# The passage from weight composition to the first batch in a four-layer residual kernel: masks asked for as their places come free, and a reordered first group

## The reference

```python
x = x + (x @ W0.T + b0 + coeff[b] * (x @ (2 * mask[b] - 1)))    # layer 0, mask[b]: 1024x1024 int32
x = x + x @ w_eff.T                                             # layer 1: w_eff from weight, scale, codebook, LoRA
x = x + (x @ W2 + b2 + 2.0 * (x @ A2[tok]) @ B2[tok])           # layer 2 (W as 'bti,io')
x = x + 1.0 * ((x @ B3[tok].T) @ A3[tok].T)                     # layer 3
```

## Time and profile before

| | us |
|---|---|
| median of 3 executions | 548.01 |
| lowest, highest | 547.4, 548.13 |
| the profiled execution | 548.42 |
| its span (first to last instruction) | 546.5 |
| TensorE busy in it | 531.0 |
| VectorE, ScalarE, GpSimd busy | 459.9, 351.4, 170.8 |

### The profile page before, as it was taken

The page is one execution under the profiler, slowest core; times in us unless marked ns, Lnnn a source line. Parts: engine busy times, 40 slices in busy tenths (PEclk is TensorE's granted clock), DMA queues, the critical chain, the costliest instruction groups (busy, mean ns, idle before and its releaser), DMA issues.

```text
span 546.5 us, 9011 instructions
## 1 busy us (share of the span) xinstructions
PE 531.0 (97%) x2864; PEld 458.3 (84%) x2864; DVE 459.9 (84%) x742; ACT 351.4 (64%) x681; POOL 170.8 (31%) x170
## 2 busy tenths in 40 slices
PE   4999999999998999999999999999999999999997
PEld 4988788888887888888888888888888888888886
DVE  5998898898963979987999889897898987989853
ACT  3777775786754874685767657667676665766730
POOL 2669878997723340003004003000300400400120
PEclk9999999999999999999999999999999999999999
DMA  8767031843487793458347455746834645564222
GB/s 231 244 90 153 21 119 60 242 140 116 98 192 259 243 355 60 151 194 165 134 143 187 94 177 170 119 151 194 164 135 156 169 110 174 170 103 156 76 50 77
DMA packets 147281, 82.57 MB, mean 151 GB/s; under 512 B 105060, under 2 KB 124516, under 8 KB 147124
## 3 DMA queue, kind: packets, MB, share of 16 engines
q1 hardware_dynamic: 145444, 78.34, 51.5%
q0 software_dynamic: 1520, 3.86, 2.7%
q10 hardware_dynamic: 288, 0.01, 0.0%
HBM read 65.93 MB, written 16.26 MB: 150 GB/s over the span
## 4 chain that ended last, share of the span: by engine, by line
PE 78%; DVE 13%; ACT 4%; DMA 3%; issue 1%; POOL 0%; SPq 0%; DVEq 0%; ACTq 0%; POOLq 0%
PE bank L1698 19%; PE bank L1705 10%; PE bank L1572 5%; PE bank L1574 5%; PE bank L1573 5%; PE bank L1742 5%; PE bank L1741 5%; PE bank L1740 5%; PE bank L1791 3%; PE bank L1789 3%; PE bank L1790 3%; DVE merged_ring L1226 3%; PE bank L1753 2%; PE bank L1482 2%; DVE m_lo L1232 1%; DVE w_lo L1133 1%
## 5 line engine op out<-in xcount | busy, mean ns | idle before, releaser
L1698 PE MATMUL bank<-x_t_pair,m_hi 128*128 128x512 f32 x512 | 128.6, 393 | 2.5 <-ACT m_hi L835 2.5
L615 POOL TENSOR_TENSOR x_t_pair<-x_sum,x_t_pair 128x256 fp32r<-128x256 f32 x32 | 29.8, 958 | 283.7 <-ACT x_t_pair L910 283.7
L1698 PEld LDWEIGHTS bank<-x_t_pair,m_hi 128*128 128x128 f32 x512 | 92.5, 189 | 20.2 <-ACT m_hi L835 3.3
L835 ACT CAST m_hi<-merged_ring 128x512 fp32r<-128x512 f32 x128 | 73.0, 619 | 55.0 <-PE bank L1705 28.0
L1232 DVE TENSOR_TENSOR m_lo<-merged_ring,m_hi 128x512 fp32r<-128x512 f32 x128 | 84.5, 708 | 9.1 <-ACT m_hi L835 9.0
L825 ACT ACTIVATE merged_ring<-mask_ring,batch_now 128x1024 f32<-128x1024 int32 x62 | 75.5, 1242 | 19.7 <-DMA mask_ring<-in_mask_Bx4096x_ik 18.7
L1226 DVE TENSOR_TENSOR merged_ring<-merged_ring,w_t 128x1024 f32<-128x1024 f32 x64 | 75.9, 1212 | 14.2 <-ACT merged_ring L825 10.7
L1705 PEld LDWEIGHTS bank<-x_t_pair,m_lo 128*128 128x128 f32 x512 | 69.8, 190 | 5.0
L1705 PE MATMUL bank<-x_t_pair,m_lo 128*128 128x256 f32 x512 | 71.4, 282 | 0.0
L1742 PE MATMUL bank<-P_hi,x_t_pair 128*128 128x496 f32 x160 | 61.4, 384 | 0.0
L1741 PE MATMUL bank<-P_lo,x_t_pair 128*128 128x496 f32 x160 | 61.4, 384 | 0.0
(11 more groups left out here) (223 smaller groups left out, 1115.0 us busy)
## 6 DMA issues: line engine op xcount, KB each, us to landing
mask_ring<-in_mask_Bx4096x_ik SPq DMA_DIRECT2D x62, 512.0 KB, 4.0
w_nat<-in_L_cond_W SPq DMA_DIRECT2D x14, 512.0 KB, 5.1
x_t_squares<-in_x SPq DMA_DIRECT2D x56, 128.0 KB, 2.9
w_raw<-in_L_cond_weight SPq DMA_DIRECT2D x16, 256.0 KB
out<-out_staged SPq DMA_DIRECT2D x16, 248.0 KB, 4.8
w0t_dram<-w_out SPq DMA_DIRECT2D x14, 256.0 KB, 3.0
w_t<-w0t_dram SPq DMA_DIRECT2D x6, 512.0 KB, 6.4
g_batch<-g_dram POOLq DMA_DIRECT2D x21, 128.0 KB, 4.2
```

Of the source, the lines that this page charges most:

```text
L835: nc.scalar.copy(Mh[:, n % MR], ring_f[:, k % MR, h * HALF:(h + 1) * HALF]).then_inc(s["h_set"], 1)
L1698: mm(bank[L0_BANK[HT * h + j]][:, :], Mh[:, n % MR, j * P:(j + 1) * P], xThl[:, :, :, k + i, :], start=(k + i == 0), stop=False, skip_grou ...
```

## The change

It moves instructions and changes five numbers of waits; nothing is computed otherwise.

- SP: mask pair 3 is asked for right after pair 1 (its own wait stays), pair 5 right after the store of W0's last half, before pair 2, and pair 4 last. The `w0t` loads ask for the exact number of used blocks of their column half, and go out in the order 0, 4, 1, 2, 3.
- ACT: the copy of W0's last half goes ahead of the last `w1_hi`; `signs(0, 2)` ahead of the x copies, whose first two wait for block 3 instead of 4 and whose last two for block 4 instead of 5; `signs(0, 3)` ahead of `m_hi(0, 0)`; `p_hi(7, [0])` behind `m_hi(0, 1)`.
- DVE: `w0_eye` ahead of the last `w1_lo`; `merged(0, 0)` between the two `x_lo_first`; `m_lo(0, 1)` ahead of `p_lo(7, [0])`.
- POOL: its two x parts wait for `p_used` too.
- First group: ACT does `p_hi(0, [0])` ahead of `mid_up(4)` and `a3_set(0)` right after P's other parts; DVE does `p_lo(0, [0])` between the last two terms of half 4.

```diff
@@ load_w0t
-                sp.wait_ge(s["p_used"], KT * (G - 1) + (4 * last + 16) // 5)
+                end = 4 * last + (10 if j < HT else 12)
+                sp.wait_ge(s["p_used"], KT * (G - 1) + (end + 4) // 5)
@@ sync
             load_mask(0, 1)
+            sp.wait_ge(s["w0_tr"], 2 * (G - 1))
+            load_mask(0, 3)
             sp.wait_ge(s["eff_set"], 2 * G)
             load_mask(0, 0)
             store_w0t(blk, 1)
+            sp.wait_ge(s["p_used"], KT * (G - 1))
+            sp.wait_ge(mask_in[1], 16)
+            load_mask(0, MR + 1)
             for h in range(2):
                 sp.wait_ge(w0_out_stored[h], 16 * (G - 1))
             load_mask(0, 2)
...
-            for j in range(HT):
+            for j in (0, HT, 1, 2, 3):
                 load_w0t(j)
@@ gpsimd
                 pool.wait_ge(s["xt_hi"], i + 1)
+                pool.wait_ge(s["p_used"], KT * (G - 1) + i + 2)
@@ scalar, half(n)
                 scaled(n - 1)
+                if n == 4:
+                    p_hi(0, range(1))
                 mid_up(n)
                 if n == 4:
-                    p_hi(0)
+                    p_hi(0, range(1, 3))
+                    a3_set(0)
...
                 w1_hi(n - 1)
-                if n == 4:
-                    a3_set(0)
@@ vector, terms_up(n)
                 term(5, term_c[:, :]).then_inc(s["terms"], 1)
+                if n == 4:
+                    p_lo(0, range(1))
@@ vector, half(n)
                 if n == 4:
-                    p_lo(0)
+                    p_lo(0, range(1, 3))
```

More of the change, by code:

```diff
@@ L424, in _ @@
             load_mask(0, 2)
-            sp.wait_ge(s["w0_tr"], 2 * (G - 1))
-            load_mask(0, 3)
             sp.wait_ge(s["w1_ready"], 2 * G)
@@ L430, in _ @@
             load_mask(0, MR)
-            sp.wait_ge(s["p_used"], KT * (G - 1))
-            sp.wait_ge(mask_in[1], 16)
-            load_mask(0, MR + 1)
-            for j in range(HT):
+            for j in (0, HT, 1, 2, 3):
                 load_w0t(j)
@@ L473, in first_batch @@
                 for k in range(MR):
-                    load_w0t(k + MR)
+                    if k:
+                        load_w0t(k + MR)
                     if k > 1:
@@ L812, in _ @@
             scaled(2 * G - 1)
+            w0_evac(G - 2, 1)
             w1_hi(2 * G - 1)
-            w0_evac(G - 2, 1)
             p_hi(G - 2)
@@ L885, in _ @@
                 signs(0, k)
+            signs(0, 2)
+            act.wait_ge(s["p_used"], KT * (G - 1) + 3)
+            x_hi(0, range(2))
             act.wait_ge(s["p_used"], KT * (G - 1) + 4)
-            x_hi(0, range(2))
-            act.wait_ge(s["p_used"], KT * (G - 1) + 5)
             x_hi(0, range(2, 4))
-            signs(0, 2)
+            signs(0, 3)
             m_hi(0, 0, True)
+            m_hi(0, 1, True)
             p_hi(G - 1, range(1))
-            signs(0, 3)
-            m_hi(0, 1, True)
             signs(0, MR)
@@ L1206, in _ @@
             effective(2 * G - 1)
+            w0_eye(G - 2)
             w1_lo(2 * G - 1)
-            w0_eye(G - 2)
             dve.wait_ge(s["late_in"], 32)
@@ L1258, in x_lo_first @@
                 nc.vector.tensor_tensor(xTl[:, i % 2, ks, :], xs0[:, i % 2, ks, :], xTh[:, i % 2, ks, :].bitcast(F32), ALU.subtract).then_inc(s["xt_first"], 1)
+            dve.wait_ge(s["p_used"], KT * (G - 1) + 4)
+            x_lo_first(0)
+            merged(0, 0, True)
             dve.wait_ge(s["p_used"], KT * (G - 1) + 5)
-            x_lo_first(0)
             x_lo_first(1)
-            merged(0, 0, True)
             m_lo(0, 0)
             merged(0, 1, True)
+            m_lo(0, 1)
             p_lo(G - 1, range(1))
-            m_lo(0, 1)
             def out_add(b, i, plain=False, first=False):
```

## The result

| | before | after |
|---|---|---|
| median of 20 executions | 548.24 us | 549.79 us |
| lowest, highest | 547.4, 549.59 | 548.3, 551.37 |
| the profiled execution, its span | 548.42, 546.5 | 550.46, 548.6 |
| mean granted clock in it | 1.000 | 0.994 |

The ratio is 1.0026, with a 95% interval of 1.0018 to 1.0034: 1.4 us slower. The prediction said 545.3 us, at most 546.9, and gave "slower" a chance of 0.05. It was wrong in sign.

A forecast was written before the change was run, and what follows sets the result against it. TensorE, busy 531.0 of 546.5 us, was taken as the bound, its passage before layer 0 bound by late-started transfers. Passage 2.1 plus first group 0.6 made 2.7 us: 548.01 to 545.3 us, range 544.2 to 546.9.

The forecast's parts named there:

- The sum of bytes: Passage: bytes queued ahead of `w0t` 0, at 311 GB/s, land it 1.7 us sooner, at 173.0; 172.5 was taken.
- The first group: First group: A3's earlier copy gains 0.6 us; the 0.6 us from `P_lo` are given back at `delta`.
- From the fourth step on nothing is lost or won: Layer 0: matmuls run without a gap from the fourth step, so its gain, 2.1 us, reaches the end.
- `w0t` 0 lands at 172.5: Passage: the first `w0t` part lands at 172.5 instead of 174.7, bounds 170.3 and 174.7.
- the hole at 163: Passage: DMA engines idle from 163 to 164; earlier mask requests fill this microsecond, worth 0.3 MB.
- L: Passage: landing of `w0t` 1, put at 175.4, between 173.8 with a dry queue and 175.9 with a full one.
- R2: Rival, passage: the queue is the bound, `w0t` 4 first costs 1.7 us, total 546.2 to 547.1 us; chance 0.19.
- The store lands at about 164, mask 2 at 168: Passage: the W0 store lands at about 164, against 163.0 before, and mask 2 3.9 us later, about 168.
- R4: Rival, passage: slower; late mask 2 holds up ScalarE and the first step, deciding from 171.5 on; 549.9 us; chance 0.05.
- mask 2 + 5.2 = 173.2 < 174.86: Passage: ScalarE's work after mask 2 takes 5.2 us, ending 1.7 us before the first step's turn.
- From a landing the first `merged` takes 1.2 us (row 1.23): Passage, VectorE: `merged` takes 1.2 us after a `w0t` landing, then half of `m_hi` 0.6, before the step starts.
- Step 3 at `merged(0, 1)` + 5.8: Layer 0: step 3 starts at L + 5.8 = 181.2, from `merged` 1.2 and ScalarE's work 4.6, 0.8 us late.

The follow-up runs named there:

- SP's order alone: SP's new order of masks and `w0t` loads, on the kernel before with the first group's part of the change: ratio 0.9989.
- with VectorE's x parts: The changed kernel with GpSimd's two x parts made by VectorE, ahead of `merged(0, 0)`: ratio 1.0004 to the kernel before.
- with fillers: The changed kernel with eight matmuls that nobody reads, between the composition and layer 0: ratio 1.0028 to the kernel before.
- GpSimd's parts held back: The kernel before with the first group's change, GpSimd's x parts waiting for the first `w0t` part: ratio 1.0030, against 0.9994 without the wait.
- `signs(0, 2)` undone: The changed kernel with ScalarE's `signs(0, 2)` back behind the x copies: ratio 1.0009 to the kernel before.
- engines alone: The changed kernel with SP's order as in the kernel before: ratio 1.0008 to the kernel before.
- VectorE's order: The changed kernel with both of VectorE's x terms ahead of the first `merged`: ratio 1.0042 to the kernel before.
- passage alone: The changed kernel without the first group's part of the change: ratio 1.0044 to the kernel before.

## Why the prediction was wrong

Two steps failed. The sum of bytes had `w0t` 0 land at 172.5, and it landed at 173.84; with this alone the kernel is level with the one before (1.0004 without GpSimd's two parts). The 1.2 us of the first `merged` were 2.14, since GpSimd stood in its way; this made the kernel slower.

**The first group: right in the trace.** 0.6 put, 0.73 there, with the 0.6 of `P_lo` given back at `delta` as worked out (0.42 us of wait for `effective(3)`). In the timed runs it was 0.3 us, not told apart from nothing.

**From the fourth step on nothing is lost or won: right** for the changed kernel (360.2 us against 360.3). In the traces of the experiments the rest of the span was 360.3 to 362.0 us. Where it was long, TensorE had waits for `m_hi` that the kernel before has shorter or not at all: 0.76 us at 197.86 and 0.90 at 245.66 with both x terms and the x copies ahead, against 0.35 at 244.44 before. So a fourth step that comes sooner is not all gain, and whether the order or chance makes these waits is open.

**"`w0t` 0 lands at 172.5": wrong, mis-sized by 1.4 us.** The request went out at 166.58, as forecast (166.4). It took 7.3 us. The step that failed is the sum of bytes: I took 311 GB/s for the ten microseconds behind the hole, and they moved 230. (The sum gave 173.0; the 0.5 us that I took off had no row behind them.) Filling the hole at 163 won nothing, since SP then stood behind the store and left another at 165. The transfers asked for first became longer, the store 7.6 us and not 4.1, mask 2 4.8 and not 3.9, `w0t` 0 7.3 and not 6.5; masks 4 and 5 became shorter (7.5 and 5.4, from 8.1 and 8.9). SP's order alone brought neither `w0t` part forward. Why the DMA engines moved fewer bytes at the same busy share stays open.

**L, the landing of `w0t` 1: 175.4 put, 176.46 measured.** It was asked for at 169.17, 0.73 us sooner than before, and took 7.3 us instead of 6.1. So `w0t` 4 ahead of it cost 1.2 us, and L lies in R2's range. The Trainium skill (DMA: Bandwidth & Descriptors, "Anatomy of one DMA"), quoted for 3.2 us, gives that price for transfers that GpSimd issues. SP issues these, and this one took 7.3 us.

**"The store lands at about 164, mask 2 at 168": the first 0.6 us late, the second 1.5.** R4's mechanism was there (store behind two more masks, ScalarE behind mask 2), though at 169.5 it stood below the 171.5 that R4 asked for. The sum "mask 2 + 5.2 = 173.2 < 174.86" priced ScalarE's own chain and stopped. ScalarE did end `signs` 3 at 173.98, ahead of the end of `merged`. What it lacked is who else reads the x copies: GpSimd's two parts, which began 1.8 us later than before (172.40, 170.56).

**"From a landing the first `merged` takes 1.2 us (row 1.23)": the step that turned the sign.** A duration read from a trace in which `merged` came first was used in a schedule in which GpSimd did. In the kernel before GpSimd had been done with its parts for 1.2 us; it began a copy 0.44 us behind `merged`, which kept its 1.23 us, and the next two `m_lo` took 1.49 and not 1.29. So the sign of the turns was in that trace, unread:

```profile
170.56 3.00 POOL L620 TENSOR_TENSOR x_t_pair<-x_squares_first,x_t_pair 128x512 fp32r<-128x512 f32 x2 [16.08 <-ACT x_t_pair L845]
175.16 1.81 POOL L625 COPY w_t<-w_last 128x512 f32<-128x512 f32 x2 [1.61 <-PE bank L1574]
176.63 1.49 DVE L1232 TENSOR_TENSOR m_lo<-merged_ring,m_hi 128x512 fp32r<-128x512 f32 x2 [0.68 <-ACT m_hi L835]
```

In the changed kernel the first `merged` took 2.14. The x term moved behind it was priced at nothing and took 1.09, and delayed `m_lo` and the second `merged`, which came at 178.56; L was then no bound at all (the part had landed at 176.46). That the x term and two `m_lo` stand between the two `merged` was not in the formula for step 2 and 3: with VectorE's x parts the second `merged` came at 177.51, 3.8 us behind the first, again with its part long there. By my formula the first step would have come at 173.86 + 1.2 + 0.6 = 175.7. `merged` added 0.9, and the x term, whose end at 177.02 the first step also wanted, 0.5 more: 177.12 (in the traces with fillers and with VectorE's x parts, too, the first step starts 0.10 us behind the x term). The fourth step's 2.16 us of delay, and the 0.73 us of the first group that it swallowed, are 2.9 us; 1.2 of these are the low clock of this one execution, the other 1.7 the late start and what the same turns did to `merged(0, 1)`.

**Step 3 at `merged(0, 1)` + 5.8: right as a formula.** With `merged(0, 1)` at 178.34 in the kernel with fillers, step 3 came at 184.05, 5.7 later. Only its start was wrong.

**R2**, the queue as the bound, was the likeliest of the rivals. It held for SP's part: L lay between its 176.3 and 177.2. None of the rivals had VectorE's and GpSimd's turns. R4, the only one that said "slower", named the late mask 2 that set them up, but not them. The text said that the moved waits "put idle time in another place" and never asked which engine would meet which in that place.

## What to carry to other kernels

Moving an instruction in time changes its neighbours, and a duration from a trace holds only with the neighbours that it had. Before you move an input of GpSimd's work, lay its new stretch beside VectorE's critical instructions: where VectorE's read two inputs from SBUF, each start behind the other's costs up to the other's whole duration. Work that an engine can do in its own wait (VectorE's two x parts, 1.29 us in a gap of 1.79) cost nothing there; on GpSimd it cost 1.2 us. And count a hole in the transfers' record as lost capacity only when a run that fills it shows an earlier landing. Here it only moved.

## What the runs showed of the hardware

VectorE and GpSimd take turns by whole instructions where VectorE's read two inputs from SBUF: a `merged` of 1.23 us took 2.14 when it started 0.21 us behind a GpSimd part and 1.22 when it started 0.11 us ahead of one. A GpSimd cast that takes 0.40 us alone stood 6.08 us behind a run of such instructions without a gap. VectorE's `P_lo`, which reads one of its inputs from PSUM, kept its 0.68 us (at 179.60, in the kernel with GpSimd's parts held back) beside a GpSimd copy that ran until 180.14.

The granted clock fell to 0.50 after waits of 2.83 us (changed kernel), 2.36 (`signs(0, 2)` undone), 2.10 (engines alone), 2.01 (VectorE's order) and 1.46 (GpSimd's parts held back, with a wait of 1.04 us five microseconds sooner). It stayed at 1.00 after 2.76 us (passage alone) and 1.64 us (before). So the length of the wait alone doesn't tell. It stayed at 0.50 for six microseconds in the changed kernel (177 to 183) and for three with the engines alone (178 to 181).
